# Half of a block's scatters behind the next norm's root on GpSimd, in a windowed-attention and mixture-of-experts kernel

## The chip, the cores and the metric

The kernel runs on one core of a Trainium2 chip. The metric is the device time of one execution in microseconds (us), as the median of several runs. The core has five engines with queues of their own: TensorE (PE; its weight loads are PEld), VectorE (DVE), ScalarE (ACT), GpSimd (POOL) and SyncE (SP). They meet only at semaphores. An engine works off its queue in order, so whatever stands behind a waiting instruction waits too. This kernel is written by hand: its semaphores and the order in each queue are in the source.

## The reference, cut to what matters

2048 tokens of width 256. Attention first, with 16 heads of width 16, a window of 32 keys and 16 global tokens, then a mixture of 64 experts of which each token takes 6, beside a shared expert:

```python
x = x + attn(layernorm(x), ...)          # own norm inside, softmax over window and 16 global keys, Wo
x = x + ffn(layernorm(x), ...)
# ffn, h = the normed rows:
scores = softmax(h @ gate_w.T); w, idx = top_k(scores, 6); w = w / w.sum(-1)
pos = place of this (token, choice) in its expert's list; kept if pos < C      # C = 384
buf[expert, pos] = h[token]                                                    # 64 x 384 rows
eo = (silu(buf @ w_gate) * (buf @ w_up)) @ w_down
y[token] += eo[expert, pos] * w;  y += shared_swiglu(h)
```

## The kernel before, in words

The tokens are 16 blocks of 128 (NT = 16). Every engine runs `step(s)` for s = 0 to 16, and in one step each stage works on another block: block a = s is normed and projected, block s-1 (b1) gets its scores, block s-2 (b2) is turned and multiplied with V, block s-3 (c) gets its output projection, residual and next norm, block s-4 (d1) its router scores and choice, block s-5 (d2) its places in the expert lists and its scatters. The blocks' last stages follow after step 16 in an order written out by hand (`placed`, `rows_turned`, `scored`, ...), mixed with the shared expert's work on pairs of blocks; that part is called the drain here. GpSimd keeps running `step` up to the last block. Then 64 experts run, with rows loaded from `expert_rows` in HBM, and their results are added into two accumulators by indirect transfers.

The pieces that the change touches:

- **Residual and norm.** On VectorE `residual(c)` (L1222) adds the projection to X1 once TensorE has done it (`vo_done`), takes the moments and writes `veps` (L1228, `var_ready`). GpSimd's `root(c)` (L1624) raises it to -0.5 and writes `rstd3` (`rstd_ready`). VectorE's `rows(c)` (L1282) then writes the normed rows into XR, a ring of UN = 4 blocks.
- **Places and slots.** TensorE counts places with two small products (L630, L631; in the drain `placed`, L717, L718). They need M of the block (`m_ready`) and the running sum `Macc` of the blocks before it (`macc_ready`), which GpSimd adds (L1641). VectorE turns the places into `slot` (L1261, `slot_ready`).
- **Scatters.** GpSimd issues six indirect transfers for a block (L1651), one per choice: 128 rows of XR each go to `expert_rows` at `slot`. They count on `slot_stored[d2 % 4]`, for which `rows`, `slots` and the token copy (L1634) wait four blocks later. The first blocks' scatters also wait for the zeroing of `expert_rows` (L369).
- **Order on VectorE in a step.** Scores of b1 read from PSUM (L1312, after `s_done`, L1305) and maxima, `residual(c)`, `weights(d2)`, `marks(d2)`, `choice(d1)`, `slots(d2)`, `lists(d1)`, `rows(c)`, `attended(b2)` (L1291, after `pv_done`). In the drain: slots(12), residual(14), choice(13), lists(13), attended(15), rows(14), marks(13), slots(13), residual(15), and so on.
- **Order on TensorE in a step.** Scores of b1 (L522, `s_done`), three transposes (the first is L535, which ScalarE copies to X2T at L978), PT transposes, projection to V (L606) and Wo (L612), router scores, places, PT transposes, q and k (L502), products with V (L660, `pv_done`).
- After the last scatter GpSimd counts `routed`; SP then loads rows of the first experts (L401), and TensorE turns them (L833).

Of the kernel before, what the change touches and what calls it, by code (L numbers as in the profile page):

```python
# [32 lines left out]
NT = T // P  # L33
# [6 lines left out]
RG = 4  # L40
NJ = H // RG
HV = HD + 1
EX, TOPK, F, FS = 64, 6, 176, 352
# [63 lines left out]
def build(nc, x, glob, ln_s, ln_b, wq, wk, wv, wo, gate, w1, w2, shg, shu, shd, out):  # L107
# [4 lines left out]
    with ExitStack() as ctx:  # L112
# [3 lines left out]
        def sem(name):  # L116
            return ctx.enter_context(nc.semaphore(name))
# [127 lines left out]
        s_done, s_read = sem("s_done"), sem("s_read")  # L245
        max_ready, exp_ready = sem("max_ready"), sem("exp_ready")
        pt_done, pt_evac, pv_done = sem("pt_done"), sem("pt_evac"), sem("pv_done")
# [54 lines left out]
        LB, LP, LC, LD, LE, LF = 1, 2, 3, 4, 5, 6  # L302
# [10 lines left out]
        def live(b):  # L313
            return 0 <= b < NT
# [51 lines left out]
        def zero_piece(engine, t, k):  # L366

            dst = rows.rearrange("(e t p) r -> t e (p r)", t=TPE, p=P)[t].rearrange("e (h w) -> e h w", h=2)
            return engine.dma_start(dst[:, :, k * ZW:(k + 1) * ZW], zero[:, :])  # L369
# [1186 lines left out]
        def _(pool):  # L1556
# [59 lines left out]
                zero_piece(pool, 1, k).then_inc(tile_zeroed[1], 16)  # L1616

            def step(s):
                c, d1, d2 = s - LC, s - LD, s - LE
                def root(c):  # L1620
                    pool.wait_ge(var_ready, c + 1)
                    if c > 0:
                        pool.wait_ge(x2_ready, c)
                    pool.tensor_tensor(rstd3[:, :], veps[:, :], power[:, 0:1], ALU.pow).then_inc(rstd_ready, 1)  # L1624

                if live(c) and c < NT - 1:
                    root(c)
                if c * 2 in range(ZN):
                    for k in (2 * c, 2 * c + 1):
                        zero_piece(pool, 2, k).then_inc(tile_zeroed[2], 16)  # L1630
                if live(d1):
                    if d1 >= UN:
                        pool.wait_ge(slot_stored[d1 % UN], 96 * (d1 // UN))
                    pool.tensor_copy(XR[:, d1 % UN, META + 2 * TOPK:META + 2 * TOPK + 1], token1[:, d1:d1 + 1])\  # L1634
                        .then_inc(token_ready, 1)
                if live(d2):
                    pool.wait_ge(pos_done, d2 + 1)
                    pool.wait_ge(m_ready, d2 + 1)
                    if d2 > 0:
                        pool.wait_ge(macc_ready, d2)  # L1640
                    pool.tensor_tensor(Macc[:, :], Macc[:, :], M[:, d2 % 2, :], ALU.add).then_inc(macc_ready, 1)  # L1641
                    if d2 < TPE:

                        pool.wait_ge(tile_zeroed[d2], 16 * ZN)
                    pool.wait_ge(slot_ready, d2 + 1)
                    pool.wait_ge(wts_ready, d2 + 1)
                    pool.wait_ge(token_ready, d2 + 1)
                    for k in range(TOPK):
                        if c == NT - 1 and k == TOPK // 2:
                            root(c)  # L1650
                        pool.indirect_dma_start(rows, bass.IndirectOffsetOnAxis(ap=slot[:, d2 % UN, k:k + 1], axis=0),  # L1651
                                                XR[:, d2 % UN, :], None, bounds_check=EX * CAP - 1,
                                                oob_is_err=False).then_inc(slot_stored[d2 % UN], 16)

            steps(step)
            for t in range(UN):
                pool.wait_ge(slot_stored[t], 96 * NT // UN)
# [113 lines left out]
```

## Time and profile before

| | |
|---|---|
| median of 3 runs | 583.54 us (579.89 to 585.85) |
| span of the profiled execution | 671.0 us |
| TensorE busy | 601.8 us (90%) |
| VectorE, ScalarE, GpSimd busy | 367.1, 282.8, 350.8 us |
| scatters of the routing (L1651) | 96, 95.2 us, mean 991 ns |
| roots (L1624) | 16, 9.1 us; 107.3 us idle before them |

The profile is one execution, recorded by the hardware's profiler. All times of rows are in microseconds from the start of its span; "idle before" is the time that the engine stood still ahead of the row, with what is taken to have released it. "remote" there names a release that the profile has no instruction for, "issue" a time in which the engine waited for nothing that the profile shows.

### The profile page before, as it was taken

The page shows a single profiled execution, that of the slowest core. Times are in us where ns is not written, and L with a number is a line of the kernel's source. Part 1 is how long each engine was busy: PE and PEld are TensorE (multiplying, and loading weights), DVE is VectorE, ACT ScalarE, POOL GpSimd, SP SyncE. Part 2 cuts the span into 40 slices and gives each one's busy share as a digit, 9 for nine tenths or more (in the row PEclk, how much of TensorE's full clock was granted, in tenths as well). Part 3 has the DMA queues.
Part 4 walks back from the last instruction along what each step waited for, and adds up shares of the span by engine and source line. Part 5 has one row for each costly group of instructions (what it writes and reads, how often), then busy time and mean ns, then how long its engine had stood idle before and what let it go on. Part 6 is the DMA issues. An engine that isn't in the chain of part 4 may idle for free. (4 is left out here: it accounts for less than half of the span.)

```text
span 671.0 us, 14628 instructions
## 1 busy us (share of the span) xinstructions
PE 601.8 (90%) x4263; PEld 490.9 (73%) x4263; DVE 367.1 (55%) x1099; ACT 282.8 (42%) x835; POOL 350.8 (52%) x344
## 2 busy tenths in 40 slices
PE   8899888778686878779999999999999999999983
PEld 7789777667565767668887777777777777777763
DVE  5878355555555564757455554545454554545425
ACT  3889245665555455612123333333333333333320
POOL 5363243332434443366326576666666666666655
PEclk9799679766667787779999999999999999999987
DMA  9999984431111111122339999999999999999667
GB/s 311 401 376 398 363 328 165 122 130 52 58 57 64 64 63 55 43 76 92 117 79 241 226 237 225 234 228 224 229 226 231 224 231 224 234 223 238 132 157 257
DMA packets 75472, 128.09 MB, mean 191 GB/s; under 512 B 15201, under 2 KB 50849, under 8 KB 72353
## 3 DMA queue, kind: packets, MB, share of 16 engines
q0 software_dynamic: 27072, 54.84, 33.5%
q1 hardware_dynamic: 46208, 67.66, 32.1%
q10 hardware_dynamic: 2144, 5.00, 2.0%
q8 instruction: 26, 0.43, 0.3%
q14 instruction: 22, 0.17, 0.1%
HBM read 65.13 MB, written 63.18 MB: 191 GB/s over the span
## 5 line engine op out<-in xcount | busy, mean ns | idle before, releaser
L1665 POOL DMA_INDIRECT acc_a<-YE,dest x64 | 99.5, 1555 | 74.8 <-ACT YE L1114 56.5
L846 PE MATMUL PS<-XET,W 128*128 128x256 f32 x512 | 127.4, 392 | 0.0
L1651 POOL DMA_INDIRECT expert_rows<-XR,slot x96 | 95.2, 991 | 57.9 <-issue 30.1
L1665 POOL DMA_INDIRECT acc_b<-YE,dest x64 | 99.4, 1553 | 46.5 <-ACT YE L1114 34.7
L846 PEld LDWEIGHTS PS<-XET,W 128*128 128x128 f32 x512 | 92.2, 189 | 30.6 <-issue 16.3
L1114 ACT ACTIVATE YE<-PS,wsel 128x256 f32<-128x256 f32 x128 | 53.8, 471 | 101.4 <-PE PS L865 96.7
L1484 DVE TENSOR_TENSOR HE<-SL,PS 128x256 f32<-128x256 f32 x64 | 26.9, 421 | 108.0 <-issue 80.7
L940 ACT ACTIVATE SMX<-SMX,smax 128x112 f32<-128x112 f32 x256 | 75.0, 393 | 0.3 <-DVE smax L1326 0.3
L862 PE MATMUL PS<-W,HE 128*128 128x256 f32 x256 | 65.9, 380 | 1.0 <-ACT YE L1114 1.0
L850 PE MATMUL PS<-XET,W 128*112 128x256 f32 x256 | 65.7, 379 | 0.0
L1624 POOL TENSOR_TENSOR rstd<-veps,power 128x1 f32<-128x1 f32 x16 | 9.1, 571 | 107.3 <-DVE veps L1228 107.3
L1475 DVE COPY XET<-PS 128x512 f32<-128x512 f32 x64 | 44.1, 691 | 27.9 <-PE PS L833 25.8
L1102 ACT ACTIVATE SL<-PS 128x256 f32<-128x256 f32 x64 | 24.6, 384 | 79.5 <-PE PS L846 65.5
L589 PE MATMUL PS<-ident,SMX 128*112 128x128 f32 x240 | 42.3, 333 | 17.3 <-issue 14.7
L1312 DVE SCALAR_TENSOR_TENSOR SMX<-PS,mask 128x448 f32<-128x448 f32 x64 | 36.0, 616 | 34.8 <-remote 31.2
L522 PE MATMUL PS<-KW,QT 32*128 32x112 f32 x512 | 43.7, 309 | 9.8 <-issue 9.1
L850 PEld LDWEIGHTS PS<-XET,W 128*112 128x112 f32 x256 | 45.3, 177 | 9.1
L589 PEld LDWEIGHTS PS<-ident,SMX 128*112 128x112 f32 x240 | 34.6, 166 | 20.9 <-issue 20.1
L862 PEld LDWEIGHTS PS<-W,HE 128*128 128x128 f32 x256 | 43.7, 190 | 4.8 <-issue 1.4
L522 PEld LDWEIGHTS PS<-KW,QT 32*128 32x128 f32 x512 | 35.5, 204 | 15.3 <-issue 14.4
L865 PE MATMUL PS<-W,HE 48*128 48x256 f32 x256 | 45.0, 428 | 0.0
L606 PE MATMUL PS<-wv_s,xnT 128*128 128x256 f32 x64 | 25.4, 537 | 16.5 <-ACT xnT L990 16.5
(179 smaller groups left out, 980.8 us busy)
## 6 DMA issues: line engine op xcount, KB each, us to landing
expert_rows<-zero POOLq DMA_DIRECT2D x24, 1088.0 KB, 14.6
W<-in_w SPq DMA_DIRECT2D x64, 368.0 KB
XG<-expert_rows SPq DMA_DIRECT2D x64, 272.0 KB
W<-in_w SPq DMA_DIRECT2D x64, 128.0 KB
W<-in_w SPq DMA_DIRECT2D x128, 48.0 KB
acc_a<-zero ACTq DMA_DIRECT2D x1, 2048.0 KB, 14.3
acc_b<-zero ACTq DMA_DIRECT2D x1, 2048.0 KB, 18.3
SMX<-acc_a POOLq DMA_DIRECT2D x4, 512.0 KB, 6.5
```

The costliest lines, as they stand in the source:

```text
L522: mm = pe.matmul(S_ps[:, g, NB * k + w, :], QT[r, b1 % 2, k, w].rearrange("p e q -> p (e q)"), KW[r, b1 % 2, k, w, :], start=True, stop=True)
L589: mm = pe.transpose(PT_ps[:, n, k, :], SM[:, b2 % 2, NJ * n + k, :], ident[:, :])
L846: mm = pe.matmul(PS[:, 2 + q, u * MAIN:u * MAIN + n], W1[:, j, d, u * P:(u + 1) * P], XET[:, q, d, 0:n], start=(d == 0), stop=(d == DC - 1))
L850: mm = pe.matmul(PS[0:W1C - 2 * P, TAIL[q], 0:n], W1[:, j, d, 2 * P:W1C], XET[:, q, d, 0:n], start=(d == 0), stop=(d == DC - 1))
L862: pe.matmul(PS[:, 5 + t, c], HE[:, q, 0, t * P:(t + 1) * P], W2[:, j, 0, :], start=True, stop=False)
L865: mm = pe.matmul(PS[:, 5 + t, c], HE[r, q, 1, t * P:(t + 1) * P], W2[r, j, 1, :], start=False, stop=True)
L940: i = act.activation(SM[:, b % 2, h], SM[:, b % 2, h], ACT.Exp, bias=smax[:, b % 2, h:h + 1])
L1114: act.mul(YE[:, e.slot, t, :], PS[:, 5 + t, e.odd * D:(e.odd + 1) * D], wsel[:, e.slot, t:t + 1]).then_inc(y_ready, 1)
L1312: dve.scalar_tensor_tensor(out=sm, in0=sp_, scalar=SM_SCALE, in1=mk, op0=ALU.mult, op1=ALU.add).then_inc(s_read, 1)
L1475: dve.tensor_copy(XET[:, e.odd, :, 0:n], PS[:, e.odd, :].rearrange("p (c n) -> p c n", c=DC)[:, :, 0:n]).then_inc(et_evac, 1)
L1651: pool.indirect_dma_start(rows, bass.IndirectOffsetOnAxis(ap=slot[:, d2 % UN, k:k + 1], axis=0), XR[:, d2 % UN, :], None, bounds_check=EX ...
L1665: pool.indirect_dma_start(target, bass.IndirectOffsetOnAxis(ap=dest[:, e.slot, t:t + 1], axis=0), YE[:, e.slot, t, :], None, bounds_check= ...
```

## The change

Only GpSimd's queue changes. Before, the root of block c stood at the head of step c + 3, ahead of the token copy, Macc and the six scatters of block c - 2, except for block 15, whose root stood in the middle of block 13's scatters. Now the roots of blocks 0, 1 and 2 stay at the head of their steps, and every later root, block c + 1 seen from step c + 3, stands in the middle of the scatters of block c - 2, one step earlier in program order; so block 15's stands among block 12's. Also, the first scatter of a block waits for `s_done` of block s - 1, or, for block 13, for `pv_done` of the last block.

```diff
             def step(s):
-                c, d1, d2 = s - LC, s - LD, s - LE
+                b1, c, d1, d2 = s - LB, s - LC, s - LD, s - LE
...
-                if live(c) and c < NT - 1:
+                if c == 0 and c < NT - 1:
+                    root(c)
+                if 0 < c <= LE - LC:
                     root(c)
...
                     pool.wait_ge(token_ready, d2 + 1)
+                    if live(b1):
+
+                        pool.wait_ge(s_done, 2 * (b1 + 1))
+                    elif b1 == NT + 1:
+
+                        pool.wait_ge(pv_done, RG * NT)
                     for k in range(TOPK):
-                        if c == NT - 1 and k == TOPK // 2:
-                            root(c)
+                        if k == TOPK // 2 and live(c + 1):
+                            root(c + 1)
                         pool.indirect_dma_start(rows, bass.IndirectOffsetOnAxis(ap=slot[:, d2 % UN, k:k + 1], axis=0),
```

GpSimd's queue in the middle of the blocks, before: the step with block 9's root and block 7's scatters, up to the next root. L1624 is the root (rstd3 from veps), L1634 the token copy, L1641 Macc, L1651 the scatters, of which "x5" are five in a row.

```order
L1624 TENSOR_TENSOR rstd3<-veps,power 128x1 [waits x2_ready,var_ready]
L1634 COPY XR<-token1 128x1 [waits slot_stored0]
L1641 TENSOR_TENSOR Macc<-Macc,M 128x64 [waits macc_ready,m_ready,pos_done]
L1651 DMA expert_rows<-XR,slot 24576x272 [waits token_ready,wts_ready,slot_ready]
L1651 DMA expert_rows<-XR,slot 24576x272 x5
L1624 TENSOR_TENSOR rstd3<-veps,power 128x1 [waits x2_ready,var_ready]
```

The same place in the changed kernel, whose lines are L1636 (token copy), L1643 (Macc) and L1659 (scatters).

```order
L1659 DMA expert_rows<-XR,slot 24576x272 x3
L1636 COPY XR<-token1 128x1 [waits slot_stored0]
L1643 TENSOR_TENSOR Macc<-Macc,M 128x64 [waits macc_ready,m_ready,pos_done]
L1659 DMA expert_rows<-XR,slot 24576x272 [waits token_ready,s_done,wts_ready,slot_ready]
L1659 DMA expert_rows<-XR,slot 24576x272 x2
L1624 TENSOR_TENSOR rstd3<-veps,power 128x1 [waits x2_ready,var_ready]
```

The root has moved into the middle of the six, so three scatters of a block now stand behind the next step's root, ahead of that step's token copy and Macc.

GpSimd's queue in the drain, before: from the last root at the head of a step (block 14's) over block 12's and block 13's scatters.

```order
L1624 TENSOR_TENSOR rstd3<-veps,power 128x1 [waits x2_ready,var_ready]
L1634 COPY XR<-token1 128x1 [waits slot_stored1]
L1641 TENSOR_TENSOR Macc<-Macc,M 128x64 [waits macc_ready,m_ready,pos_done]
L1651 DMA expert_rows<-XR,slot 24576x272 [waits token_ready,wts_ready,slot_ready]
L1651 DMA expert_rows<-XR,slot 24576x272 x5
L1634 COPY XR<-token1 128x1 [waits slot_stored2]
L1641 TENSOR_TENSOR Macc<-Macc,M 128x64 [waits macc_ready,m_ready,pos_done]
L1651 DMA expert_rows<-XR,slot 24576x272 [waits token_ready,wts_ready,slot_ready]
L1651 DMA expert_rows<-XR,slot 24576x272 x2
L1624 TENSOR_TENSOR rstd3<-veps,power 128x1 [waits x2_ready,var_ready]
```

The same blocks in the changed kernel.

```order
L1636 COPY XR<-token1 128x1 [waits slot_stored1]
L1643 TENSOR_TENSOR Macc<-Macc,M 128x64 [waits macc_ready,m_ready,pos_done]
L1659 DMA expert_rows<-XR,slot 24576x272 [waits token_ready,wts_ready,slot_ready]
L1659 DMA expert_rows<-XR,slot 24576x272 x2
L1624 TENSOR_TENSOR rstd3<-veps,power 128x1 [waits x2_ready,var_ready]
L1659 DMA expert_rows<-XR,slot 24576x272 x3
L1636 COPY XR<-token1 128x1 [waits slot_stored2]
L1643 TENSOR_TENSOR Macc<-Macc,M 128x64 [waits macc_ready,m_ready,pos_done]
L1659 DMA expert_rows<-XR,slot 24576x272 [waits token_ready,pv_done,wts_ready,slot_ready]
L1659 DMA expert_rows<-XR,slot 24576x272 x5
```

Block 15's root stands six scatters, a token copy and a Macc earlier, and the second Macc of the piece (block 13's) is behind it instead of ahead.

## Rows read from the trace of the kernel before

**Rows 1.** Stretches: bounds, length, busy us of each engine, clock, DMA share, GB/s.

```profile
0.00:60.00 60.00, 54.09 (x613) 48.75 (x614) 43.60 (x113) 44.77 (x144) 28.29 (x64) 0.94 0.98 368
60.00:276.00 216.00, 171.93 (x1692) 149.42 (x1693) 119.47 (x343) 118.56 (x389) 78.98 (x104) 0.74 0.36 132
276.00:335.00 59.00, 52.95 (x346) 45.44 (x344) 35.43 (x117) 14.99 (x45) 33.56 (x42) 0.91 0.25 91
335.00:640.00 305.00, 303.97 (x1545) 232.22 (x1545) 156.35 (x516) 101.69 (x254) 193.00 (x125) 1.00 0.92 214
```

**Rows 2.** Timeline of VectorE: residuals of blocks 2 and 13 (start, us, instruction).

```profile
59.79 0.48 DVE L1222 SCALAR_TENSOR_TENSOR X<-X,res_scale,PS 128x256 f32<-128x256 f32 x1 [0.62 <-PE PS L612]
...
274.20 0.48 DVE L1222 SCALAR_TENSOR_TENSOR X<-X,res_scale,PS 128x256 f32<-128x256 f32 x1 [0.20 <-PE PS L612]
```

**Rows 3.** Stretches, columns as in rows 1: a step without and one with scatters.

```profile
49.00:59.80 10.80, 10.80 (x155) 10.34 (x153) 8.87 (x25) 10.43 (x36) 1.96 (x4) 1.00 1.01 399
183.00:201.40 18.40, 15.41 (x155) 13.28 (x153) 10.60 (x30) 11.02 (x37) 6.89 (x9) 0.72 0.17 58
```

**Rows 4.** Waits of the whole span: waiter, releaser, total us, times, longest.

```profile
POOL rstd L1624 <- DVE veps L1228: 107.3, 13, 12.3
...
ACT X2T L978 <- remote: 41.2, 7, 6.3
DVE rden L1291 <- remote: 35.3, 7, 7.4
...
DVE XR L1282 <- POOL rstd L1624: 3.3, 1, 3.3
```

**Rows 5.** Timeline of one step, block 8's residual to block 9's.

```profile
181.55 0.48 DVE L1222 SCALAR_TENSOR_TENSOR X<-X,res_scale,PS 128x256 f32<-128x256 f32 x1 [3.29 <-PE PS L612]
...
182.99 0.57 POOL L1624 TENSOR_TENSOR rstd<-veps,power 128x1 f32<-128x1 f32 x1 [7.52 <-DVE veps L1228]
183.66 0.29 POOL L1641 TENSOR_TENSOR Macc<-Macc,M 128x64 bf16<-128x64 bf16 x1
...
185.06 2.05 PE L660 MATMUL PS<-VW,PT 112*64 112x17 f32 x64
...
185.58 0.17 DVE L1261 TENSOR_TENSOR slot<-slotf,over 128x6 int32<-128x6 f32 x1
...
186.57 1.06 POOL L1651 DMA_INDIRECT expert_rows<-XR,slot  x1 [2.61 <-DVE slot L1261]
187.35 0.41 DVE L1282 TENSOR_SCALAR XR<-X,mv,rstd 128x256 f32<-128x256 f32 x1
...
190.11 0.26 DVE L1291 RECIPROCAL rden<-PS 128x16 f32<-128x16 f32 x1 [2.35 <-remote]
...
193.05 0.97 POOL L1651 DMA_INDIRECT expert_rows<-XR,slot  x1 [0.30 <-issue]
193.72 1.15 DVE L1312 SCALAR_TENSOR_TENSOR SMX<-PS,mask 128x448 f32<-128x448 f32 x2 [2.89 <-remote]
...
195.30 0.37 ACT L978 COPY X2T<-PS 128x256 f32<-128x256 f32 x1 [5.98 <-remote]
...
199.99 0.48 DVE L1222 SCALAR_TENSOR_TENSOR X<-X,res_scale,PS 128x256 f32<-128x256 f32 x1 [1.58 <-PE PS L612]
```

**Rows 6.** Timeline of the drain: block 15's residual, TensorE's placement of block 14.

```profile
300.04 0.48 DVE L1222 SCALAR_TENSOR_TENSOR X<-X,res_scale,PS 128x256 f32<-128x256 f32 x1 [0.43 <-PE PS L750]
...
304.71 0.19 PE L717 MATMUL PS<-M,tri 128*128 128x64 bf16 x1
```

**Rows 7.** Timeline: last scatter, loads of experts' rows, TensorE's first turn of them.

```profile
325.63 0.98 POOL L1651 DMA_INDIRECT expert_rows<-XR,slot  x1 [0.30 <-issue]
...
328.25 12.90 SPq L401 DMA_DIRECT2D XG<-expert_rows  x5
...
335.24 1.04 PE L833 MATMUL PS<-ident,XG 128*128 128x128 f32 x8
```

**Rows 8.** DMA issues: transfer, queue, count, KB each, median us to landing.

```profile
X<-in_x SPq DMA_DIRECT2D x1, 384.0 KB, 4.6
```

**Rows 9.** Timeline of GpSimd in the drain: block 12's Macc.

```profile
287.31 0.66 POOL L1641 TENSOR_TENSOR Macc<-Macc,M 128x64 bf16<-128x64 bf16 x1
```

## What the change is expected to do to the time

> **What bounds the kernel now.** I read the stretches of the trace first, to see which engine sets each stage. From 60 to 335 us the 16 blocks pass attention and routing, and no engine is full there: between 60 and 276 us TensorE is busy for 171.93 of 216 us at a granted clock of 0.74, VectorE and ScalarE for 119 us each, GpSimd for 79 us. From 335 to 640 us the experts run, and TensorE is busy for 303.97 of 305 us at clock 1.00. The first 60 us have the DMA engines at 0.98 [rows 1]. So only the middle can give time or take it.
>
> Second, the length of a step, which is the distance of two starts of L1222 on VectorE (the residual of a block; I call that start R). The residuals of blocks 2 and 13 start at 59.79 and 274.20 us, eleven steps apart: 19.5 us each [rows 2]. The step just before, 49.00 to 59.80, has no scatter in it and takes 10.8 us with TensorE busy all through. A step with six scatters takes 18.4 us, though VectorE works for 10.60 and ScalarE for 11.02 us in it [rows 3].
>
> Third, the waits. Much of them is called "remote": ScalarE before its copy of X2T 41.2 us in 7 waits, VectorE before rden 35.3 in 7. GpSimd waits 107.3 us for veps ahead of its root, and VectorE waited for a root just once, 3.3 us [rows 4]. That once is block 0's, ahead of any scatter.
>
> Fourth, one step in order of time. R is 181.55. The root follows 1.44 us later, the slots start at R+4.03, and the six scatters run from 186.57 to 194.02 (R+5.02 to R+12.47). TensorE's products with V are done by 187.11, but VectorE reads them at 190.11; SMX starts at 193.72; ScalarE takes X2T at 195.30, after 5.98 us of waiting. Next R is 199.99, 5.97 us behind the last scatter's end [rows 5]. While scatters run, what TensorE hands over reaches its readers late.
>
> **The profiled execution and the runs.** The span is 671.0 us, the median of the runs is 583.54: 87.5 us apart. Experts and first stage are full of TensorE's work and of transfers [rows 1] and can't hold that much, so I place nearly all of it in 60 to 335 us. The excess of eleven steps over 10.8 us is 214.4 - 118.8 = 95.6 us, and I add 12 us for the drain (276 to 335 us; its "remote" waits are part of [rows 4]): about 108 us. An ordinary run then keeps 108 - 87.5 = 20 us of it, a share of 0.19. I work each term out on the profiled execution and carry it over with that share where it is a piece of this stall, in full where it is a piece of an engine's work.
>
> **The waits that are added** (s_done, pv_done). They stand behind slot_ready on the same engine. VectorE writes the slots of block s-5 in step s (L1261) after it has read the scores of block s-1 (L1312), for which it waited for the same count of s_done (L1305). For block 13 the wait is for pv_done of the last block; VectorE writes those slots after attended(B), which waits for that count too. Both are true whenever slot_ready is. Cost 0, apart from a few waits issued while GpSimd idles for slots (2.61 us in the step shown [rows 5]).
>
> **The root between the scatters.** It waits for the residual of the block after, which is in the next step. So three scatters of a block go at once, and three only in the next step, behind the root; what queues behind that root is these three, the next token copy and Macc. Who waits for them: TensorE's placement of the next block needs the previous Macc; rows and slots reuse a ring of four blocks, two steps later than the late scatters. In step terms: root at R+1.44 for 0.57, 0.18 to the scatter behind it, three scatters 1.06 + 0.30 + 0.97 + 0.30 + 0.97 = 3.60, so R+2.2 to R+5.8; token copy and Macc until R+6.3; the slots have been ready since R+4.2, so three more from R+6.5 to R+10.1. The row of the slots was followed by its scatter 0.99 us later; R+6.5 is past that. The burst ends at R+10.1 instead of R+12.47: 2.4 us earlier. VectorE needs the root at R+5.80 (L1282), it is there at R+2.0 in both kernels: nothing gained by the root itself.
>
> If the 5.97 us from the last scatter to the next R stay, a step of the profiled execution shrinks by 2.4 us. Ten steps: 24; the first, behind block 0's slots, holds three scatters in place of six: 3 x 1.28 = 3.85. Together 27.9 us in the profiled execution. Bounds for an ordinary run: 0 (its stall is none of this) and 27.9 (all of it). By the share it is 5.3 us. I take half, 2.6 us, since the share is a difference of large numbers and the second bound below it is zero.
>
> The Trainium skill ("DMA: Bandwidth & Descriptors", Anatomy of one DMA) gives some 2.0 us fixed for a transfer issued from GpSimd, so by that estimate the late scatters have landed by about R+8, before their ring entries are reused. No row here shows the landing of a scatter.
>
> **The drain.** Block 15's root used to stand among block 13's scatters; now it is among block 12's, so from there on all of GpSimd's queue waits for R of block 15, 300.04 [rows 6]. Root at 301.48 to 302.05, three scatters of block 12 to 305.83, token copy, Macc for block 13 done at 306.3. TensorE's placement of block 14 (L717 at 304.71 [rows 6]) waits for that Macc: it moves to about 306.4, +1.7 us. TensorE is nearly gapless from there to the experts, so I count all of it. Then GpSimd needs 7.5 us of scatters each for blocks 13, 14 and 15 with token copy, Macc and dispatch between: 306.5 to 313.9, 314.6 to 322.1, 322.7 to 330.2, where the last ended at 326.61. The XG loads go from 328.25 to 331.8, and TensorE needs the first at 335.24 + 1.7 = 336.9 [rows 7]. That leaves 5.1 us for a load of 272 KB that has no landing row; a larger one, 384 KB of in_x, took 4.6 us [rows 8]. So the cover is whole, by 0.5 us at worst; without it the cost is up to 3.6 in place of 1.7.
>
> **Sum.** Profiled execution: 671.0 - 27.9 + 1.7 = 644.8 us. Ordinary runs: 583.5 - 2.6 + 1.7 = 582.6 us. One per cent, 5.8 us, is about what a measurement of this kernel can tell from no change.
>
> **Rivals.**
> Most of the stall's gain reaches the runs. For: it recurs in every step of the trace, and 20 us of it have to be left somewhere. Against: 87.5 us of it are not in the runs. At 0.4 of 27.9 it is 11.2 - 1.7 = 9.5, 574.0 us; at the whole 557.3. It decides from 0.27 on. Chance 0.24.
>
> Two bursts cost more than one. The first now meets the q/k products and the copies of QT and KW behind them, which ran free of scatters (R to R+5), and the scores follow from these. For: rden and SMX each waited anew under one burst [rows 5]. Against: VectorE's chain from weights to slots waits on little from TensorE. One microsecond a step gives 583.5 + 11 + 1.7 = 596.2 us; it decides from 0.4 us a step. Chance 0.13.
>
> GpSimd's work beside VectorE's small instructions stretches them. Twelve instructions from R+1.4 to R+4.2 now run beside the root and scatters. Where root, token copy and Macc ran beside VectorE at 287.3 us, the Macc took 0.66 us instead of 0.29 [rows 5, 9]. At 0.05 us each for VectorE it is 0.6 a step, 583.5 + 6.6 + 1.7 = 591.8. The Trainium skill ("SBUF — State Buffer", SBUF: two separate sides) calls the port that both use an exclusive lock, one fully blocks the other; the 0.66 agrees in kind. Chance 0.05.
>
> Nothing moves, the change does not do what it looks like: the waits are void and an ordinary run hides the shift: 583.5 to 585.2. This lies inside my forecast's own range, 578 to 589, with the forecast at 0.58 in all.
>
> **Numbers.** Faster by over 1%: 0.24. Within 1%: 0.58. Slower: 0.13 + 0.05 = 0.18. Range 572 to 592: it takes in the lower rival at 0.4 and the third, and cuts the tails of whole gain and of 1 us a step.
>
> **What would show it.** Right: in the changed trace two bursts of three, the first from about R+2.2, the last scatter at R+10.1; steps of 16 us; a span near 645 while the runs hardly move; L717 of block 14 idle for a Macc; last scatter 3 to 4 us later against R of block 15. Wrong: steps still of 18.4 us though the burst ends earlier (the stall isn't tied to the scatters' end); "remote" waits before QT or PT copies (second rival); runs that fall with the span (first rival); a wait for s_done ahead of a scatter.

## The result and the profile after

The changed kernel takes 591.61 us in the median of four runs (588.94 to 592.56), the kernel before 582.94 us in four runs beside them: ratio 1.013, 95% interval 1.0087 to 1.0172. It is 1.3% slower. I had forecast 582.6 us and no change; the time lies inside my outer range of 572 to 592, at its upper edge, and outside the forecast's own range of 578 to 589.

The profiled execution of the changed kernel has a span of 589.7 us. This fits its runs (a run is 1.8 us longer than its span), where the profile of before had a span of 671.0 us against runs of 583.54. Three chips were used in what follows, and I name them A, B and C. On chip A the kernel before takes 673.87 us (19 runs), on B 581.75 (19; 583.23 in a second round of 9), on C 583.49 (25). On which chips the result and the first profile were taken is not on record; by their times I take the profile that I had read to be from a chip like A, and the runs from chips like B and C. So the changed kernel's stretches are set beside a profile of the kernel before from chip C (span 577.1 us), not beside [rows 1].

Changed kernel, the stretches with columns as in [rows 1]:

```profile
60.00:200.00 140.00, 134.52 (x1772) 122.29 (x1770) 127.21 (x367) 122.47 (x406) 85.21 (x109) 0.95 0.56 205
200.00:260.00 60.00, 54.75 (x313) 46.98 (x312) 34.14 (x106) 10.55 (x30) 30.18 (x36) 0.94 0.25 89
260.00:550.00 290.00, 290.00 (x1475) 220.59 (x1474) 149.39 (x495) 98.21 (x246) 188.63 (x122) 1.00 0.96 224
```

The kernel before on chip C, the same stretches:

```profile
60.00:200.00 140.00, 136.17 (x1849) 123.32 (x1849) 127.02 (x380) 124.15 (x416) 86.94 (x116) 0.98 0.58 211
200.00:260.00 60.00, 58.43 (x291) 49.51 (x290) 36.29 (x112) 13.01 (x34) 30.43 (x34) 1.00 0.33 105
```

The blocks are done by 250 us in both, not by 335. TensorE is busy for 136.17 of 140 us in the kernel before, VectorE for 127.02. There is next to no stall to shrink. In the changed kernel TensorE is a little less busy in the steps, and much less in the drain, at a lower granted clock in both stretches. The experts' stretch is full, as it was.

The waits of the changed kernel that answer to [rows 4] (waiter, releaser, total us, times, longest):

```profile
POOL rstd L1624 <- DVE veps L1228: 48.8, 15, 8.9
...
PE PS L717 <- issue: 4.5, 2, 2.9
```

No "remote" wait is left among them, and none is in the profile of the kernel before from chip C either. L717, TensorE's placement of a block, had no wait called "issue" there. The step that answers to [rows 5] stands in the next part.

### The profile page after: what moved, and what is told of

It is laid out like the page before. It is cut to its first block and busy times, and to the rows that moved or that the text cites. A ratio compares the mean times of both kernels' runs of the same rounds, so it can differ in the third digit from the quotient of the medians.

```text
span 589.7 us, 14638 instructions
## 1 busy us (share of the span) xinstructions
PE 557.6 (95%) x4263; PEld 457.7 (78%) x4263; DVE 369.4 (63%) x1099; ACT 280.6 (48%) x835; POOL 351.8 (60%) x344
## 5 line engine op out<-in xcount | busy, mean ns | idle before, releaser
L1659 POOL DMA_INDIRECT expert_rows<-XR,slot x96 | 97.9, 1019 | 29.9 <-issue 26.4
L1492 DVE TENSOR_TENSOR HE<-SL,PS 48x128 f32<-48x128 f32 x128 | 37.2, 291 | 3.6 <-ACT SL L1104 0.9
L589 PE MATMUL PS<-ident,SMX 128*112 128x128 f32 x240 | 35.9, 295 | 2.7 <-ACT SMX L940 2.6
L833 PE MATMUL PS<-ident,XG 128*128 128x128 f32 x256 | 38.2, 273 | 0.0
L1624 POOL TENSOR_TENSOR rstd<-veps,power 128x1 f32<-128x1 f32 x16 | 9.1, 568 | 48.8 <-DVE veps L1228 48.8
L833 PEld LDWEIGHTS PS<-ident,XG 128*128 128x128 f32 x256 | 32.0, 141 | 7.2
L1104 ACT ACTIVATE SL<-PS 48x256 f32<-48x256 f32 x64 | 24.1, 377 | 26.3 <-PE PS L850 26.3
```

Source lines behind the costliest of these rows:

```text
L589: mm = pe.transpose(PT_ps[:, n, k, :], SM[:, b2 % 2, NJ * n + k, :], ident[:, :])
L833: mm = pe.transpose(PS[:, e.odd, d * MAIN + t * P:d * MAIN + (t + 1) * P], XG[:, e.slot, t, d * P:(d + 1) * P], ident[:, :])
L1492: i = dve.tensor_tensor(HE[64 * t:64 * t + FT, q, 1, c], SL[0:FT, q, 1, c], PS[64:64 + FT, TAIL[q], c], ALU.mult)
```

## The experiments

They run from the stall that the prediction rested on, over the two halves of the change, to the instructions that pay. R is the start of L1222, as before; a step is the distance of two R.

**The kernel before, profiled again (chip A).**

> The kernel before, unchanged, for a second profile: its first one has a span of 671.0 us beside runs of 583 us, the changed kernel's has 589.7 us beside runs of 591.6. If the waits named remote belong to that one execution, the span is near 581 us here and the steps are 11 to 12 us long. If they belong to the old order of the scatters, the span is again near 670 us with steps of 18.5 us.

It took 677.85 us, with a span of 676.1. The waits are those of [rows 4]:

```profile
ACT X2T L978 <- remote: 36.6, 6, 6.3
...
DVE rden L1291 <- remote: 36.3, 8, 7.4
```

As all its runs on this chip are near 674 us, the stall is in every execution there. It is no property of being profiled.

**The added waits alone (chip A, and again on chip C).** The edit to the kernel before, ahead of the six scatters:

```
-                c, d1, d2 = s - LC, s - LD, s - LE
+                b1, c, d1, d2 = s - LB, s - LC, s - LD, s - LE
...
+                    if live(b1):
+                        pool.wait_ge(s_done, 2 * (b1 + 1))
+                    elif b1 == NT + 1:
+                        pool.wait_ge(pv_done, RG * NT)
```

> The kernel before with the added waits on s_done and pv_done alone, no root moved. Both theories (drain, steps) put the loss on the moved roots and expect 583 us, ratio 1.000 within 0.4%. Rival: the waits themselves hold the scatters back, then up to the 8.7 us of the whole change show here, 588 to 592 us.

> The waits on s_done and pv_done alone, no root moved, beside the others on this chip. They are true whenever slot_ready is: ratio 1.000 within 0.4%. If they cost, the part of it is missing from the 5.4 us of the run with the changed kernel's steps, 583 to 587 us where before takes 581.8.

Chip A: 674.8 us, ratio 1.0019 (0.9979 to 1.0059). Chip C: 582.53, ratio 0.9974 (0.9948 to 0.9999). The waits cost nothing that can be seen on either.

**The changed steps with the drain as before (chip A, and again on chip B).** The edit to the changed kernel:

```
-                if 0 < c <= LE - LC:
+                if 0 < c <= LE - LC or c == NT - 2:
                     root(c)
...
-                        if k == TOPK // 2 and live(c + 1):
+                        if k == TOPK // 2 and c + 1 < NT - 2:
                             root(c + 1)
+                        if k == TOPK // 2 and c == NT - 1:
+                            root(c)
```

> The changed kernel with the roots of blocks 14 and 15 put back where they stood before, so that the drain's queue on GpSimd is the old one and blocks 3 to 13 have the new order. Drain theory (the Macc of blocks 12 and 13 stand behind the root and three scatters; in the changed kernel's trace TensorE waits 1.68 and 2.86 us at L717 and its next eight matmuls take 3.76 instead of 1.89 us): nearly all is back, 583 to 585 us. Step theory (the loss is spread over the eleven steps): nothing is back, 590 to 592 us.

> The version with the changed kernel's steps and the drain as before, again, beside the changed kernel on the same chip. Drain theory: 583 to 585 us where the kernel before takes 583, and 6 to 9 us below the changed kernel on any chip. Step theory: within 2 us of the changed kernel.

Chip A: 670.45 us, ratio 0.996 (0.9925 to 0.9996), 3.4 us less. Chip B: 587.13, ratio 1.0088 (1.005 to 1.0126), 5.4 us more. The same steps win a little on the one chip, hardly beyond the measurement, and lose on the other. On chip A the burst does end where I had put it, and TensorE stands still elsewhere. Timeline of that step on chip A, R at 174.65, a row being a run of instructions of one line:

```profile
177.68 1.39 PE L660 MATMUL PS<-VW,PT 112*64 112x17 f32 x39
...
179.59 0.21 PE L660 MATMUL PS<-VW,PT 112*64 112x17 f32 x1 [0.51 <-issue]
...
183.82 0.98 POOL L1661 DMA_INDIRECT expert_rows<-XR,slot  x1 [0.30 <-issue]
...
184.15 3.49 PE L522 MATMUL PS<-KW,QT 32*128 32x112 f32 x32
...
192.41 0.48 DVE L1222 SCALAR_TENSOR_TENSOR X<-X,res_scale,PS 128x256 f32<-128x256 f32 x1 [1.49 <-PE PS L612]
```

The last scatter ends at 184.80, R+10.1 as predicted. The products with V (L660) took 2.05 us in one piece in [rows 5]; here they are torn into pieces with gaps of 0.4 to 0.5 us that wait for nothing the profile shows, and the scores behind them take 3.49 us. From the last scatter to the next R it is 7.6 us, not the 5.97 that I had let stay. This step of 17.76 us is one of the shorter ones: in the trace steps of 17.7 and of 19.7 to 20.0 us alternate, and in the one before it, with R at 154.92, the last scatter ends at R+10.2 too and the next R is 9.6 us behind it.

**Each Macc ahead of the three late scatters (chip A).** In the changed kernel the Macc goes right behind the root:

```
-                    pool.tensor_tensor(Macc[:, :], Macc[:, :], M[:, d2 % 2, :], ALU.add).then_inc(macc_ready, 1)
+                    if d2 == 0 or not live(c):
+                        add_marks(d2)
...
                             root(c + 1)
+                            add_marks(d2 + 1)
```

(add_marks is Macc with its three waits, which move with it.)

> The changed kernel with each Macc moved ahead of the three late scatters, right behind the root that it follows; the scatters stay split. Drain theory: TensorE's waits at L717 shrink by the 4 us of three scatters each, so about 585 us or less, though the last scatter still ends as late as in the changed kernel. If it is the late end of the scatters (last one 30 us behind block 15's residual) that costs, the time stays at 590 to 592 us.

It took 690.24 us, ratio 1.0263 (1.0179 to 1.0347), slower by more than either expectation allowed. Its trace shows L660 torn again, now with gaps of 1.0 to 1.2 us:

```profile
201.84 0.27 PE L660 MATMUL PS<-VW,PT 112*64 112x17 f32 x2 [1.17 <-issue]
```

Between 60 and 190 us such gaps in L660 come to 25.1 us here and to 21.5 us in the kernel one above. Why they are longer here is open. It says nothing on chips without the stall.

**The changed kernel again (chip B).**

> The changed kernel itself. On the chip of the first four runs the kernel before takes 674 us and shows waits named remote, on the chip of the result 583 and none in the changed kernel's trace. If this is a chip that takes 583 us for the kernel before, the ratio is again 1.013. If it is one that takes 674: the version with the drain as before had 0.996 there, and with 6 to 9 us for the drain on top the changed kernel comes to 677 to 680 us, ratio 1.005 to 1.009. The prediction's step term (27.9 us earlier by the burst's end) would give 648 us.

592.07 us, ratio 1.0165 (1.0084 to 1.0246), span 588.2: the loss repeats, 10.3 us.

**The drain alone (chip B).** In the kernel before only the roots of blocks 14 and 15 move into the scatters of blocks 11 and 12:

```
-                if live(c) and c < NT - 1:
+                if live(c) and c < NT - 2:
...
-                        if c == NT - 1 and k == TOPK // 2:
-                            root(c)
+                        if k == TOPK // 2 and c + 1 in (NT - 2, NT - 1):
+                            root(c + 1)
```

> The kernel before with only the roots of blocks 14 and 15 moved into the scatters of blocks 11 and 12: the drain of the changed kernel behind the steps of the kernel before. Drain theory: it loses most of what the changed kernel loses, 6 to 9 us (589 to 592 us on a chip that takes 583 before). Step theory: it loses less than 2 us.

586.41 us, ratio 1.008 (1.0045 to 1.0114): 4.7 us. With the 5.4 of the steps alone this is 10.1, and the whole change costs 10.3 on the same chip (8.7 in the result): the halves add up, as far as intervals of 2 us on each half and 5 us on the whole can tell. The timeline of TensorE in the drain of the changed kernel:

```profile
206.86 0.19 PE L717 MATMUL PS<-M,tri 128*128 128x64 bf16 x1 [1.68 <-issue]
...
217.06 0.21 PE L717 MATMUL PS<-M,tri 128*128 128x64 bf16 x1 [2.86 <-issue]
...
217.14 3.76 PE L688 MATMUL PS<-X2T,shu_s 128*128 128x256 f32 x8
```

and of the kernel before on chip C:

```profile
202.37 0.19 PE L717 MATMUL PS<-M,tri 128*128 128x64 bf16 x1
...
209.39 0.19 PE L717 MATMUL PS<-M,tri 128*128 128x64 bf16 x1
...
210.24 1.99 PE L688 MATMUL PS<-X2T,shu_s 128*128 128x256 f32 x8 [0.63 <-DVE SH L1394]
```

GpSimd in the changed kernel at the same two places:

```profile
206.44 0.32 POOL L1643 TENSOR_TENSOR Macc<-Macc,M 128x64 bf16<-128x64 bf16 x1
...
211.78 0.57 POOL L1624 TENSOR_TENSOR rstd<-veps,power 128x1 f32<-128x1 f32 x1 [1.28 <-DVE veps L1228]
...
216.65 0.32 POOL L1643 TENSOR_TENSOR Macc<-Macc,M 128x64 bf16<-128x64 bf16 x1
```

Each L717 starts 0.1 us behind the end of a Macc: block 12's, which has the root of block 14 and three scatters ahead of it, and block 13's, behind the root of block 15 and three more. The eight products behind the second wait then take 3.76 us for 1.99: the granted clock is 0.50 from 217.10 to 220.95, the lower of its two levels, and 1.00 in the kernel before from 210.20 to 212.30. The kernel with the drain alone shows the same three things (1.45, 2.85, and 3.44 for the eight), and takes 60.2 us from block 13's R to the first L833, where the kernel before takes 55.2 (chip C).

**The kernel before, profiled on chip C.**

> The kernel before, unchanged, for a profile on whatever chip this is. If the chip takes about 582 us, the steps from block 5 to block 13 are 10.83 us apart with VectorE busy without a gap, as in the run with only the drain changed, and no wait is named remote. If it takes 674, the profile is again that of rows 5.

578.8 us, span 577.1. One step of it, R to R 10.84 us, with VectorE's instructions behind the slots and GpSimd beside them (the profile's scatter line here is L1651, Macc L1641):

```profile
120.87 0.47 DVE L1222 SCALAR_TENSOR_TENSOR X<-X,res_scale,PS 128x256 f32<-128x256 f32 x1
...
123.16 0.30 POOL L1641 TENSOR_TENSOR Macc<-Macc,M 128x64 bf16<-128x64 bf16 x1
...
125.09 0.17 DVE L1265 CAST XR<-topi 128x6 f32<-128x6 uint32 x1
...
125.87 1.06 POOL L1651 DMA_INDIRECT expert_rows<-XR,slot  x1 [2.41 <-DVE slot L1261]
...
126.19 0.19 DVE L1273 TENSOR_TENSOR half<-half 128x64 bf16<-128x64 bf16 x1
...
126.64 0.41 DVE L1282 TENSOR_SCALAR XR<-X,mv,rstd 128x256 f32<-128x256 f32 x1
...
131.71 0.47 DVE L1222 SCALAR_TENSOR_TENSOR X<-X,res_scale,PS 128x256 f32<-128x256 f32 x1
```

And one of the changed kernel, R to R 11.21 us:

```profile
133.30 0.47 DVE L1222 SCALAR_TENSOR_TENSOR X<-X,res_scale,PS 128x256 f32<-128x256 f32 x1
...
136.82 0.98 POOL L1659 DMA_INDIRECT expert_rows<-XR,slot  x1 [0.30 <-issue]
...
137.51 0.28 DVE L1265 CAST XR<-topi 128x6 f32<-128x6 uint32 x1
...
138.10 1.14 POOL L1659 DMA_INDIRECT expert_rows<-XR,slot  x1 [0.30 <-issue]
...
138.71 0.37 DVE L1273 TENSOR_TENSOR half<-half 128x64 bf16<-128x64 bf16 x1
...
139.34 0.52 DVE L1282 TENSOR_SCALAR XR<-X,mv,rstd 128x256 f32<-128x256 f32 x1
139.38 0.31 POOL L1643 TENSOR_TENSOR Macc<-Macc,M 128x64 bf16<-128x64 bf16 x1
...
144.51 0.47 DVE L1222 SCALAR_TENSOR_TENSOR X<-X,res_scale,PS 128x256 f32<-128x256 f32 x1
```

R needs no wait in either: VectorE has a next instruction at hand through the whole step. Three of its instructions have become longer, 0.11, 0.18 and 0.11 us, in sum 0.40; the step is 0.37 longer. The busy sums of such a step, before (chip C) and changed (the one behind the step shown), columns as in [rows 1]:

```profile
120.87:131.71 10.84, 10.74 (x152) 9.63 (x150) 10.22 (x32) 10.42 (x37) 6.89 (x10) 1.00 0.29 99
```

```profile
144.51:155.71 11.20, 10.80 (x152) 9.62 (x150) 10.58 (x32) 10.39 (x37) 7.14 (x9) 1.00 0.29 97
```

VectorE's sum has grown by 0.36 us, as the step has, TensorE's by 0.06 with the same 152 products, and GpSimd's, which is idle for 4 us of the step, by 0.25. TensorE fills the step of the kernel before as well as VectorE does; in the changed step shown it waits 0.17 us for L1282. Beside the three instructions now run the second and third late scatter and the Macc; this Macc used to be over by R+2.6. The traces of both versions with these steps on chip B have the same three at 278 to 280, 362 to 363 and 513 to 516 ns.

**The root ahead of the sixth scatter (chip C).** In the kernel with the drain as before:

```
-                        if k == TOPK // 2 and c + 1 < NT - 2:
+                        if k == TOPK - 1 and c + 1 < NT - 2:
```

> Steps with the root ahead of the sixth scatter instead of the fourth (five scatters at once, one late), drain and queue of the last roots as before. In the changed kernel's steps three instructions of VectorE behind the slots (L1265, L1273, L1282) take 0.28, 0.37 and 0.52 us instead of 0.17, 0.19 and 0.41, since late scatters, token copy and Macc of GpSimd end beside them; with one late scatter they end by R+3.8, ahead of L1265 at R+4.2. Theory of the overlap: steps of 10.85 us again, 581 to 583 us where before takes 581.8 (three late ones: 587.1). Rival, the split as such costs: 586 to 588 us.

582.75 us, ratio 0.999 (0.9955 to 1.0025). The split burst costs nothing that can be seen when only one scatter is late, and the step is 10.8 us again. The groups of VectorE by line, from 110 to 188 us (busy us, mean ns of one, idle before), first in the changed kernel, then with one late scatter:

```profile
L1282 DVE TENSOR_SCALAR XR<-X,mv,rstd 128x256 f32<-128x256 f32 x7 | 3.6, 512 | 0.3
...
L1273 DVE TENSOR_TENSOR half<-half 128x64 bf16<-128x64 bf16 x7 | 2.6, 365 | 0.2
...
L1265 DVE CAST XR<-topi 128x6 f32<-128x6 uint32 x7 | 2.0, 281 | 0.2
```

```profile
L1282 DVE TENSOR_SCALAR XR<-X,mv,rstd 128x256 f32<-128x256 f32 x7 | 2.9, 412 | 0.3
...
L1273 DVE TENSOR_TENSOR half<-half 128x64 bf16<-128x64 bf16 x7 | 1.3, 192 | 0.2
...
L1265 DVE CAST XR<-topi 128x6 f32<-128x6 uint32 x7 | 1.2, 172 | 0.2
```

The second fence is what the kernel before has too (412, 192, 173 ns).

**The drain alone, with its two Macc ahead of the late scatters (chip C).** To the kernel with the drain alone:

```
                         if k == TOPK // 2 and c + 1 in (NT - 2, NT - 1):
                             root(c + 1)
+                            add_marks(d2 + 1)
```

Their old place, at the head of the step, is left out for these two blocks (`if c not in (NT - 2, NT - 1): add_marks(d2)`).

> Only the drain changed, as in the run that took 586.4 us, but with the Macc of blocks 12 and 13 ahead of the three late scatters, right behind the root. Theory (TensorE's placement waits for the Macc, 1.45 and 2.85 us, and its next matmuls run at the lower clock, 3.44 for 1.99 us): 581 to 583 us. Rival, it is the scatters' late end or the queue as a whole: still 585 to 588 us.

582.97 us, ratio 0.9986 (0.9958 to 1.0015). The 4.7 us are gone, though the roots still stand where the change puts them and the scatters still end late. TensorE's rows:

```profile
206.72 0.19 PE L717 MATMUL PS<-M,tri 128*128 128x64 bf16 x1
...
213.74 0.19 PE L717 MATMUL PS<-M,tri 128*128 128x64 bf16 x1
```

The last scatter ends 30.0 us behind R of block 15, as late as in the changed kernel (30.3). This settles the drain: its cost is the Macc behind the late scatters, by the waits of L717 and what follows from them. (The two versions ran on different chips, B and C, each beside the kernel before; from block 13's R to the first L833 this one takes 55.4 us.)

**The root ahead of the fifth scatter (chip B).** As with the sixth, with TOPK - 2.

> The steps of the changed kernel with the root ahead of the fifth scatter (four at once, two late), the last two roots where they were before. With three late, three VectorE instructions were longer in each step: the cast of L1265 (0.28 for 0.17 us) whose time falls in the last 0.3 us of the second late scatter, the product of L1273 (0.37 for 0.19) in the last part of the third, and L1282 (0.52 for 0.41) beside token copy and Macc; with one late, none was. If it is the scatters' and Macc's position beside just these instructions: with two late the cast of L1265 still falls on the end of the second late scatter and takes 0.28 us; the third late scatter is gone, the token copy and Macc stand at R+4.6 to R+5.1, so L1273 and L1282 take 0.19 and 0.41. The step is 10.95 us, ten of them 1.1 us longer than before, ratio about 1.002. If instead it is the waits of the late scatters for the next slots or the split of the burst as such: step 11.2, all three longer, ratio about 1.009.

588.84 us, ratio 1.0097 (1.0061 to 1.0134): as much as with three late, so my sum for this version, 1.002, was wrong. Most steps are 11.20 us. But the split as such does not explain it either, for other instructions pay (R at 124.89):

```profile
128.71 0.23 DVE L1256 SCALAR_TENSOR_TENSOR slotf<-XR,place 128x6 f32<-128x6 f32 x1
...
128.97 0.23 DVE L1261 TENSOR_TENSOR slot<-slotf,over 128x6 int32<-128x6 f32 x1
...
129.44 0.57 DVE L1270 TENSOR_TENSOR hot<-iota_e,XR 128x384 bf16<-128x384 f32 x1
129.53 0.64 POOL L1643 TENSOR_TENSOR Macc<-Macc,M 128x64 bf16<-128x64 bf16 x1
...
130.33 1.01 POOL L1661 DMA_INDIRECT expert_rows<-XR,slot  x1 [0.16 <-issue]
130.34 0.22 DVE L1273 TENSOR_TENSOR half<-half 128x64 bf16<-128x64 bf16 x1
...
130.82 0.63 DVE L1282 TENSOR_SCALAR XR<-X,mv,rstd 128x256 f32<-128x256 f32 x1
```

L1256 and L1261, beside the second late scatter, take 0.23 us each for 0.17, and L1265 its usual 0.17. The Macc meets L1270 and takes 0.64 us; the first scatter for the new slots comes at R+5.44 instead of R+5.00, and L1282, which used to start 0.77 us into that scatter and take 0.41, now starts 0.49 into it and takes 0.63. With 0.03 on L1273 the four have grown by 0.06, 0.06, 0.03 and 0.22 us, 0.37 in sum, and the step by 0.36. So it matters what an instruction of VectorE meets on GpSimd. How far into a scatter it starts does not decide it alone: L1256 took 0.23 us here, 0.30 into one, and 0.17 in the changed kernel's step, 0.29 into one. On chips B and C no version with a moved root is faster than the kernel before.

## Why the prediction was wrong

**The share of the stall: the step that failed.** I had a span of 671.0 and runs of 583.54 us, put the 87.5 us between them down to a stall that an ordinary run keeps 0.19 of, and carried -2.6 us over. The measured price of the steps is +5.4 us (chip B). The runs of a chip don't keep a share of the stall: those of chip A have it whole, and a profile from chip C shows a step of 10.84 us with no wait for anything "remote". The rows told of it: the step without scatters was 10.8 us, and in one with scatters VectorE was busy for 10.60 and ScalarE for 11.02 us [rows 3], so a step without the stall has no room much below 10.8 us, and nothing was left for the change to win. The 20 us that I let the runs keep were no stall. On chip C the eleven steps take 124.8 us, not 118.8 (the first two are 14.1 and 12.9), and from block 13's R to the first L833 the stalled trace has 61.0 us against 55.2, so 5.8 more and not 12. That is 12 of the 20; most of the rest is that I set a span against a median of runs (583.5, where the span on chip C is 577.1).

The busy sums alone don't say which engine then sets the step (chip C: TensorE 10.74 us, ScalarE 10.42, VectorE 10.22). The versions do: in the changed steps and in those with two late scatters the step grows by what VectorE's instructions grow, 0.37 for 0.40 and 0.36 for 0.37, and with one late scatter neither grows. VectorE has no slack, and what lengthens its instructions is a cost that my sum did not have.

**The stall itself.** Where it is, the predicted 27.9 us became 3.4 (chip A). The burst ended at R+10.1, but what follows took 7.6 or 9.6 us instead of 5.97. I had expected steps of 16 us; the eleven from block 2's to block 13's R take 205.9 us in this trace, 18.7 each, against 212.2 in the second profile of the kernel before. That the steps stay long though the burst ends earlier was my own sign of being wrong.

**The third rival was the mechanism, at another place.** I gave it 0.05 and looked at the twelve instructions from R+1.4 to R+4.2. The timeline shows none of them longer. The late scatters, token copy and Macc reach to R+6.4, and what pays is L1265, L1273 and L1282, behind the slots: 0.37 us a step, not 0.6.

Nine steps from block 4's to block 13's R, which takes 97.7 us in the kernel before (chip C) and 102.6 in the changed one, hold 9 x 0.37 = 3.3 of the 4.9 us. The rest goes with two steps of some 12 us in the changed kernel's trace, whose L1222 waits for TensorE (1.6 us in all between 88 and 192, against 0.3 before) at a lower granted clock, 0.86 in the one from 109.85 to 122.08. The four traces with steps of 11.2 us off chip A have two or three steps of 11.6 us or more behind block 4's R; the five with steps of 10.84 have one or none. With a longer step TensorE idles more: 10.80 of 11.20 us busy against 10.74 of 10.84. That this idling lowers the clock is argued, not shown. It is luck that this rival's 591.8 us stands so near the measured 591.61: it had 6.6 us for the steps and 1.7 for the drain, where chip B shows 5.4 and 4.7.

The Trainium skill ("SBUF — State Buffer", SBUF: two separate sides) lets whichever of the two engines started first keep the shared port pair for its whole instruction, on VectorE's side for an instruction in a two-port mode or with two inputs in SBUF. The Macc of 0.64 us that began 0.09 behind L1270 agrees in kind; that a scatter lengthens only some of the instructions beside it, and those by 0.06 to 0.22 us, is not what a lock for the whole of a scatter would give.

**The drain: right place, mis-sized.** Term: +1.7 for one placement that waits for one Macc. Measured: 4.7 us alone (chip B). I had asked only what queues behind block 15's root. Block 14's had moved by the same rule, so the Macc of block 12 is late as well, 1.68 us, and block 13's by 2.86; the eight products behind the second gap take 1.8 us more. 1.68 + 2.86 + 1.77 = 6.3; the kernel before has 0.63 there for another reason, and the changed kernel's trace is 5.9 us longer from block 13's R to the first L833 (61.1 against 55.2). My 1.7 was measured from the stalled profile's L717 [rows 6], to which TensorE came late: 4.67 us behind R of block 15, where chip C's trace has 3.70.

**Right.** The added waits: no cost, twice. The end of the split burst at R+10.1: 143.44 - 133.30 in the changed kernel. The cover of the XG loads, which I had thought thin by [rows 7, 8], is 8 us:

```profile
239.72 0.97 POOL L1659 DMA_INDIRECT expert_rows<-XR,slot  x1 [0.30 <-issue]
...
242.34 1.79 SPq L401 DMA_DIRECT2D XG<-expert_rows  x4
...
250.44 1.04 PE L833 MATMUL PS<-ident,XG 128*128 128x128 f32 x8
```

Of the second rival little is seen: ahead of the q copies (L958) the waits between 60 and 190 us come to 2.2 us, against 1.1 in the kernel before on chip C. The first rival's gain did not come, since there was nothing to gain from.

## What to carry to other kernels

Before a term is priced from a profile, hold its span against the times of the runs; where they differ by more than the ends of the program explain, the profile is of another state of things, and its waits are no measure of what the runs can win. The busy sums of the engines in a step are the better guide to that; which of several nearly full engines sets the step takes an experiment that lengthens one of them. Work moved on GpSimd has two prices besides its own time: each small result queued behind it (here a Macc that TensorE needs; ask it for every moved instruction, not for the last), and each instruction of VectorE that it newly runs beside, once VectorE is the bound. If a root has to stand inside a burst, let the small result go right behind it, and keep the late part short enough to be over when the next chain starts. The first took the drain's loss away here; in the steps it was tried on chip A alone, where it made things worse. The second took the steps' loss away.

## What the hardware showed that I had not expected

The same kernel takes 674 us on one chip and 582 to 583 on two others. In the traces of the first, the eleven steps from block 2's to block 13's R take 212 to 214 us in the kernel before, for 124.8 on chip C, and in them TensorE halts or its results reach their readers late, with gaps that wait for nothing shown; with the root moved the gaps move into L660 (21.5 us in the seven steps between 60 and 190 us), with the Macc moved too they come to 25.1. What it is in that chip is open; no run here took the scatters away, so that scatters are the cause is not shown either.

A scatter of one microsecond lengthens some of its neighbours on VectorE and not others: L1282 started 0.77 us into one and took 0.41, 0.49 into one and took 0.63; L1273 started 0.32 into one and took 0.19, 0.61 into one and took 0.37. The third late scatter, beside L1273, itself took 1.14 for 0.98. What decides between the two is open; the start within the scatter alone does not (L1256, above).

After 2.86 us without work at L717, eight products of L688 took 3.76 us instead of 1.99, at a granted clock of 0.50 instead of 1.00. After the 1.68 us at the L717 before, the clock stayed at 1.00, and eight products took 1.89. The gap costs more than its own length.
